# Transposing the next group's rows around the last two down products of an MLP group

## The reference, cut to what matters

```python
x = x + o                                   # o: output of the delta-rule part
h2 = x * rsqrt(mean(x * x) + 1e-6) * mlp_norm_w
gate = h2 @ Wgate.T                         # 512 -> 1408
up = h2 @ Wup.T                             # 512 -> 1408
x = x + (silu(gate) * up) @ Wdown.T         # 1408 -> 512
```

## Time and profile before

| | |
|---|---|
| median of 3 runs | 3121.78 us (3118.45 to 3122.65) |
| the profiled execution | 3120.97 us |
| its span in the trace | 3119.2 us |
| TensorE busy over the span | 2773.0 us (89%) |
| VectorE busy | 1992.1 us (64%) |
| ScalarE busy | 1437.7 us (46%) |
| mean granted TensorE clock | 0.93 |

### The profile page before, as it was taken

How to read it: one execution, slowest core, us unless ns; L and a number is a source line. 1 busy time by engine, 2 the same in 40 slices (tenths; PEclk the granted TensorE clock), 3 DMA queues, 4 the chain that set the end, 5 groups by cost and what they waited for, 6 DMA issues and landing times. The chain is left out here.

```text
span 3119.2 us, 66716 instructions
## 1 busy us (share of the span) xinstructions
PE 2773.0 (89%) x26968; PEld 1468.7 (47%) x26968; DVE 1992.1 (64%) x2991; ACT 1437.7 (46%) x2378; POOL 1008.6 (32%) x713
## 2 busy tenths in 40 slices
PE   6999999686888888988747999999999799999997
PEld 2444444252453444544424444444444366666664
DVE  3444444459989889898892444445552377777776
ACT  2222222484776767757613322222222256666664
POOL 0000000116527438255390000000000077777776
PEclk9999999887988988989866999999999899999999
DMA  6999889400000000000121022322210111111110
GB/s 239 336 332 334 300 305 313 145 15 1 2 29 2 29 29 2 29 10 21 62 107 42 26 96 81 108 95 95 73 64 27 62 35 40 40 40 40 40 44 31
DMA packets 126284, 290.20 MB, mean 93 GB/s; under 512 B 30480, under 2 KB 35216, under 8 KB 121968
## 3 DMA queue, kind: packets, MB, share of 16 engines
q1 hardware_dynamic: 122608, 261.85, 24.1%
q10 hardware_dynamic: 3456, 25.17, 2.4%
HBM read 244.96 MB, written 42.01 MB: 92 GB/s over the span
## 5 line engine op out<-in xcount | busy, mean ns | idle before, releaser
L2123 POOL TENSOR_TENSOR d_zb<-d_za 128x1024 f32<-128x1024 f32 x32 | 75.3, 2354 | 987.6 <-DVE d_za L2185 987.6
L899 PE MATMUL b_e<-b_hT,s_region 128*128 128x512 f16 x1152 | 283.1, 392 | 47.4 <-DVE s_region L1327 36.5
L1629 PE MATMUL c_r<-c_hT,c_g_pair 128*128 128x512 f16 x1056 | 255.7, 394 | 13.1 <-DVE c_hT L1792 13.1
L1803 DVE SCALAR_TENSOR_TENSOR c_av<-c_r,c_sg 128x512 f32<-128x512 f32 x88 | 60.9, 692 | 301.6 <-PE c_r L1629 241.3
L1990 PE MATMUL d_m<-s_region,d_xiT 128*128 128x512 bf16 x1024 | 237.7, 383 | 6.5 <-ACT d_sg L2075 2.0
L1629 PE MATMUL c_r<-c_hT,c_u_pair 128*128 128x512 f16 x1056 | 243.0, 380 | 0.0
L1629 PE MATMUL c_d<-c_d_pair,c_aT 128*128 128x512 f16 x1056 | 241.0, 379 | 0.0
L1327 DVE SCALAR_TENSOR_TENSOR s_region<-b_e,b_cw,s_region 128x496 f32<-128x496 f32 (+2 forms) x288 | 203.1, 716 | 18.2 <-ACT s_region L1117 9.8
L851 POOL TENSOR_TENSOR b_tmp<-b_L,s_hn 128x496 f32<-128x496 f32 (+30 forms) x124 | 122.6, 988 | 262.0 <-ACT b_L L1100 252.6
L851 POOL TENSOR_TENSOR b_tmp<-b_L,b_U 128x496 f32<-128x496 f32 (+30 forms) x124 | 130.7, 1054 | 223.8 <-ACT b_L L1100 214.4
L899 PEld LDWEIGHTS b_e<-b_hT,s_region 128*128 128x128 f16 x1152 | 103.9, 99 | 188.4 <-DVE s_region L1327 44.2
(11 more groups left out here) (255 smaller groups left out, 6033.0 us busy)
## 6 DMA issues: line engine op xcount, KB each, us to landing
a_cT<-in_ctxT SPq DMA_DIRECT2D x128, 512.0 KB, 9.7
a_cn<-in_ctx SPq DMA_DIRECT2D x128, 512.0 KB, 9.0
a_x_ln<-in_x SPq DMA_DIRECT2D x8, 1024.0 KB, 15.9
a_cw<-in_ctx SPq DMA_DIRECT2D x128, 64.0 KB, 9.6
a_x_res<-in_x SPq DMA_DIRECT2D x32, 256.0 KB, 11.5
x<-a_x_out SPq DMA_DIRECT2D x32, 256.0 KB, 11.3
b_xg<-x SPq DMA_DIRECT2D x8, 1024.0 KB, 5.5
om<-b_hT SPq DMA_DIRECT2D x32, 256.0 KB, 2.0
```

Of the source, the lines that this page charges most:

```text
L899: mm = pe.matmul(p[:], w_qkv[:, a, i, n, c * P:(c + 1) * P], hp[:, b, n, :], start=(n + a + b == 0), stop=(n == DC - 1 and a == 1))
L1629: mm = pe.matmul(out, x, y, start=start and i == 0, stop=stop and i == 2)
L1803: V.scalar_tensor_tensor(av[:], p[:], AS / (WS * HS), sg[:, f % 2, :], ALU.mult, ALU.mult)\
L2123: nc.gpsimd.tensor_tensor(o[:, :, 0, :], a[:, :, 0, :], a[:, :, 1, :], ALU.add).then_inc(bf, 1)
```

## The change

The row work becomes three functions of their own: `rows` (PE), `high_rows` (ACT) and `low_rows` (DVE). For group 0 they run at the start, as before. For group g + 1 they are now called inside group g: PE transposes `h0` and `h1` between the up product of f = 10 and `down(9)`, and `h2` and `h3` between `down(9)` and `down(10)`. ACT and DVE do their halves after their part of f = 10, which on DVE is ahead of the four group sums. The wait for `h3` at the head of a group stays. No instruction is added or removed, and the order in which the ring's banks are used is the same.

```diff
--- before.py
+++ after.py
@@ -1629,13 +1629,17 @@
                     mm = pe.matmul(out, x, y, start=start and i == 0, stop=stop and i == 2)
                 return mm
 
-            def body(g, last):
-                for c in range(DC):
+            def rows(g, cs):
+                for c in cs:
                     p, full = R.open(pe, g, f"h{c}")
                     for t in range(TG):
                         pe.wait_ge(hn_ready, g * TG + t + 1)
                         mm = pe.transpose(p[:, t * P:(t + 1) * P], hn[:, t, c * P:(c + 1) * P], ident[:])
                     mm.then_inc(full, 1)
+
+            def body(g, last):
+                if g == 0:
+                    rows(0, range(DC))
                 R.used(pe, g, f"h{DC - 1}")
 
                 def down(f):
@@ -1661,10 +1665,14 @@
                             mm = pairs(p[:], lambda i: w[:, i, k, f * P:(f + 1) * P], lambda i: hT[:, i, k, :],
                                        k == 0, k == DC - 1)
                         mm.then_inc(full, 1)
+                    if f == FC - 1 and not last:
+                        rows(g + 1, (0, 1))
                     if f:
                         down(f - 1)
                     if (g, f) in TOTAL:
                         total(TOTAL[g, f])
+                if not last:
+                    rows(g + 1, (2, 3))
                 down(FC - 1)
 
             def total(i):
@@ -1705,11 +1713,14 @@
 
             highs(0, (0,))
 
-            def body(g, last):
+            def high_rows(g):
                 for c in range(DC):
                     p, _ = R.take(act, g, f"h{c}")
                     A.activation(hT[:, 0, c, :], p[:], ACT.Copy, scale=vec[:, c:c + 1]).then_inc(h_hi, 1)
+
+            def body(g, last):
                 if g == 0:
+                    high_rows(0)
                     highs(0, (1, 2))
                 for f in range(FC):
                     p, free = R.take(act, g, f"g{f}")
@@ -1731,6 +1742,8 @@
                             row_roots(g - 1)
                         if not last:
                             squares(g + 1)
+                if not last:
+                    high_rows(g + 1)
 
             def row_roots(g):
                 act.wait_ge(mv_ready, TG * (g + 1))
@@ -1785,13 +1798,16 @@
 
             lows(0, (0,))
 
-            def body(g, last):
+            def low_rows(g):
                 for c in range(DC):
                     p, free = R.take(dve, g, f"h{c}")
                     dve.wait_ge(h_hi, g * DC + c + 1)
                     V.scalar_tensor_tensor(hT[:, 1, c, :], p[:], vec[:, c:c + 1], hT[:, 0, c, :],
                                            ALU.mult, ALU.subtract).then_inc(free, 1)
+
+            def body(g, last):
                 if g == 0:
+                    low_rows(0)
                     lows(0, (1, 2))
                 for f in range(FC):
                     R.used(dve, g, f"g{f}")
@@ -1822,6 +1838,8 @@
                             rows_out(g - 1)
                         if not last:
                             normalise(g + 1)
+                if not last:
+                    low_rows(g + 1)
                 dve.wait_ge(xt_ready, TG * (g + 1))
                 dve.wait_ge(stored, 16 * TG * g)
                 for t in range(TG):
```

## The result

The changed kernel takes 3091.27 us (median of 4 runs, 3087.47 to 3099.6), the kernel before 3122.22 (4 runs, 3118.45 to 3125.74). The ratio is 0.9905, with a 95% interval from 0.9881 to 0.9929. Forecast were 3090 us, a range from 3083 to 3103, and a gain. Executions of one kernel spread over up to 12 us here, so I read the parts of the sum from the traces, not from the medians.

A forecast was written before the change was run, and what follows sets the result against it. TensorE, busy for 720.66 of 760 us in the MLP stage, was taken as the bound. Shorter boundaries (21.2 us) and the kept clock (10.9) sum to 32.1 us off the median of 3121.78: 3090 us, range 3083 to 3103.

The forecast's parts named there:

- At fixed clock: Seven boundaries between groups, each 2.57 us beside its two down products where it was 5.55: 21.2 us saved.
- The stall at `h1`: New TensorE wait before transposing `h1`, until VectorE's `c_av` frees the bank of `u10`: 0.81 us per boundary.
- The two waits of today: TensorE's idle times for low halves, 1.56 us at `h2` and 1.64 us before the first gate product: both gone.
- the zero: Time origin of the forecast's boundary: the end of the last up product's issue on TensorE, 1785.35 in the old trace.
- Group sums and loads: VectorE's sums end 2.7 us into the next group, loads are issued some 6.5 us later: nothing waits.
- The clock: First gate products of groups 1 to 7 stay at 2.4 GHz, which gives back 10.9 us.
- the first: Rival, chance 0.14: the clock falls as now in five boundaries of seven; saving 21.2 us alone, 3100.6 us.
- the third: Rival, chance 0.05: the clock falls at every boundary, transposes and stall together being a hole; saving 14.5 us, 3107 us.
- the slower one: Rival, chance 0.04: clock falls at the stall until after the first gate product, 8.7 us per boundary; 3151 us.
- the handovers didn't cost more: Rival, chance 0.05: longer `h1` stall or late low halves, 1.0 us more per boundary; 3097 us, or 3108 with clock lost.
- the idle time didn't just move: Rival, chance 0.02: stalls at `h1` and later reach 3.8 us per boundary, nothing won; about 3120 us.
- Idle time or transposes: Step claiming the clock fell after TensorE's idle time in the boundary, not after the transposes; basis for 10.9 us.

The follow-up runs named there:

- VectorE's order alone: The kernel before with the next group's four low halves ahead of the group sums on VectorE, TensorE and ScalarE unchanged: 3124.83 us (1 run).
- The filler kernel: The kernel before with six matmuls into a spare bank, result unread, after `h1` and after `h3` in each boundary: 3112.07 us, ratio 0.9951.
- the kernel with the longer stall: The changed kernel with three useless VectorE additions between `c_av` of f = 10 and the release of its bank: 3121.22 us (1 run).

## Why the prediction was right

*At fixed clock: 21.2 us forecast, 22.1 measured.* A boundary was to cost 2.57 us beside its two products. It costs 7.61 - 5.18 = 2.43, and 2.54 in the first. Seven of them are 17.1 us, against 39.21 in the earlier trace rows.

*The stall at `h1`: 0.81 forecast.* It is 1786.55 - 1785.37 - 0.44 = 0.74 us in the first boundary and 0.62 in the others, 0.57 and 0.46 as the profile shows it. The step that priced the hand-over by the spacing of the group sums was a little high: PE resumed 0.81 us after the start of `c_av` (1786.55 against 1785.74), where 0.88 was forecast. In the other boundaries `c_av` also starts earlier, 0.26 us after the issue's end in the second (1874.45 against 1874.19) and 0.37 in the first.

*The two waits of today are gone.* Shown by the waits view: no wait of TensorE for low halves is left outside group 0. In the first boundary the two pairs of low halves end 4.26 and 7.10 us after the zero (4.1 and 7.1 forecast). Three parts were tested, and each is needed: VectorE's order alone gives 5.0 us, 2.65 of them idle time and the rest from one boundary more that kept its clock; without the second pair's place on TensorE 14.2 are missing; with two low halves behind the sums all of it.

*Group sums and loads cost nothing.* Sums end 2.5 us into the next group (2.7 forecast) and the load is issued 3 us into it. `lifted` begins behind its cast with no wait. The 8.5 us that the prediction took for the slowest load are a median; nothing depended on it.

*The clock: 10.9 us forecast, 11.4 to 11.6 measured.* The filler kernel gives 11.4 us of stage for it alone. In the changed kernel 705.60 - 739.51 = -33.9 us less 22.1 of idle time and 0.15 in group 0's first product leaves 11.6. The forecast left out that in three groups the up product's first matmuls were slow too, 0.2 to 0.3 us each. The 5 of 7 boundaries that it started from are the count in one execution, and the same idle times could also give another: the kernel with VectorE's order alone lost 4 at nearly the same ones. So the size of this term is less certain than the sum makes it look.

*The rivals.* The clock fell in no boundary, so the first, the third and the slower one are out as forecasts for this kernel. The stall was shorter than forecast and no second wait came, so the handovers didn't cost more and the idle time didn't just move. The slower rival was also mispriced, since it let the low clock last through 36 matmuls: in the kernel with the longer stall it lasted through 12.

*Idle time or transposes.* The prediction said that the clock fell for the idle time and not for the transposes. That step isn't settled. The rule of the Trainium skill ("TensorE: Matmul & The Clock Gate", Part 4) that transpose-mode work doesn't bring the full clock did no harm here: sixteen transposes lie in each boundary, and the clock read 1.00 in all seven. But in its boundaries the changed kernel never goes without f16 matmuls for more than 1.7 us, so it couldn't show the rule either, and in the kernel with the longer stall, where that stretch is 3.6 us, the clock fell at every boundary. No run here shows whether transposes alone would raise the clock.

*The total.* The stage gave 33.9 us and the span fell by 31.5. The other 2.4 came in the stages around it: 0.2 before group 0's first product, 1.0 at the hand-over to the FFN (15.5 us from the last matmul to the first, where it was 14.5) and 1.2 within the FFN. The hand-over takes one of these two values, to within 0.2 us, in all nine traces, among them 15.51 in a kernel with the old order on TensorE, and the FFN stage varies over 2.8 us with the same code. So these aren't effects of the change. What sets the hand-over to one value or the other was not tried. That the total came so near the forecast (31.5 us in the span, 30.95 between the medians, 32.1 forecast) is therefore partly luck: the two terms were 0.9 and 0.7 us too small, and the stages around took 2.4 back.

## What to carry to other kernels

Where the busiest engine stops at the seam between two groups for a chain through other engines, put the head of the next group's chain in front of the last pieces of work that need nothing from it, one link per piece, and check the order on every engine of the chain: one link behind the wrong work on VectorE undid the whole gain. Price a seam with idle time twice, once as the idle time and once as the slower clock after it; filler work into a spare bank measures the second price by itself. If the moved work needs a resource that was released only just now, split the work in front of it to cover the release.

## What the runs showed of the hardware that was not expected

How often the clock fell doesn't go by the total of idle time in a boundary. 0.27 + 0.34 us and 0.46 us: never. 0.46 and 1.86 us with 24 matmuls of 512 columns between them: never. 1.24 + 1.64 us with eight transposes between: 4 of 7. 1.56 + 1.64: 5 of 7. 3.11 in one piece, with 0.46 earlier: 6 of 7. 2.54 in one piece, between groups of four transposes: 7 of 7. So two idle periods with only transposes between them brought the clock down, though each was shorter than the 1.86 us that never did. Measured from the last f16 matmul to the next, transposes included, the longest stretch was 1.9 us or less in the kernels with 0.46 us alone, none, or fillers, and 2.89 in the one with 1.86, where the clock held; it was usually 3.28, 3.63, 5.22 and 5.55 in those where it fell in 6, 7, 4 and 5 of 7 boundaries. These runs don't tell the two accounts apart, and with seven boundaries in one trace each the counts are rough.

At the same idle times the product behind them took 2.76 us in some boundaries and 4.45 or 5.30 in others. The two slow lengths differ in when the clock fell. In the kernel before it had fallen during the wait ahead of the three products of 5.30 us (it reads 0.50 from 1888.40 to 1889.60 in the second boundary), and they were slow from the first matmul to the last. Ahead of the two of 4.45 us it still read 1.00 over the whole boundary; it fell in their first 0.3 us and was back 0.6 us or more before their end. What decides when it falls, or whether it does, in one and the same kernel is open.

The clock came back by itself in the last matmuls of the first slow product or in the first ones behind it, wherever that product stood: 1.3 to 2.5 us were lost in it, and never more than 0.5 us behind it.
